# Turning the attention keys on the vector engine from a second, split read, in place of the tensor engine

## What is computed

```python
x = x + xattn(layernorm(x), ctx, ctx, Wq, bq, Wk, bk, Wv, bv)
#   qp = q @ Wq + bq; kp = ctx @ Wk + bk; vp = ctx @ Wv + bv
#   softmax(qp @ kp.T / sqrt(512)) @ vp
x = x + attn(layernorm(x), ...)     # q, k per head normalised, sigmoid gate, @ Wo + bo
x = x + ffn(layernorm(x), ...)      # one of 8 experts per row
```

## Time and profile before

| | |
|---|---|
| median of 3 runs | 393.93 us |
| span of the profiled execution, first to last instruction | 391.0 us |
| time of the runs less that span | 2.8 to 3.7 us, 2.9 for the median |
| PE busy | 363.3 us, 93% of the span |
| PE weight loads | 232.2 us |
| DVE busy | 147.2 us, 38% |
| ACT busy | 93.3 us, 24% |
| POOL busy | 82.2 us, 21% |
| moved by DMA | 56.48 MB in 13798 packets, mean 144 GB/s |

### The profile page before, as it was taken

The page is one execution under the profiler, slowest core; times in us unless marked ns, Lnnn a source line. Parts: engine busy times, 40 slices in busy tenths (PEclk is TensorE's granted clock), DMA queues, the critical chain, the costliest instruction groups (busy, mean ns, idle before and its releaser), DMA issues.

```text
span 391.0 us, 6077 instructions
## 1 busy us (share of the span) xinstructions
PE 363.3 (93%) x2346; PEld 232.2 (59%) x2346; DVE 147.2 (38%) x341; ACT 93.3 (24%) x191; POOL 82.2 (21%) x87
## 2 busy tenths in 40 slices
PE   1999999999999999999999999999889989799993
PEld 1786667435646544565654455653435869697781
DVE  4100365003616523351652444342362654155322
ACT  2222321213215331222541222241302400000000
POOL 4000243500215002022400201202322402511122
PEclk9999998999999999999999999999999999899998
DMA  7999200399700029710004950000693052920000
GB/s 256 409 404 351 93 0 2 107 341 373 309 2 0 2 80 382 264 27 0 0 0 174 380 200 0 2 0 2 230 421 157 3 214 71 324 104 18 29 24 25
DMA packets 13798, 56.48 MB, mean 144 GB/s; under 512 B 1574, under 2 KB 1606, under 8 KB 9680
## 3 DMA queue, kind: packets, MB, share of 16 engines
q1 hardware_dynamic: 11776, 50.35, 34.3%
q0 software_dynamic: 2000, 5.83, 4.2%
HBM read 53.03 MB, written 4.19 MB: 146 GB/s over the span
## 4 chain that ended last, share of the span: by engine, by line
PE 83%; DVE 6%; issue 3%; POOL 3%; ACT 2%; DMA 2%; DVEq 0%; ACTq 0%; POOLq 0%; SPq 0%
PE TR L911 14%; PE A L916 13%; PE ST L1005 12%; PE SC L982 12%; PE A L1191 8%; PE A L936 4%; PE A L958 4%; PE TR L916 4%; PE SC L1173 3%; PE A L911 2%; PE SC L1148 1%; DMA AW_sb<-rows,idxg_sb 1%; PE TR L992 1%; PE A L1123 1%; PE A L1053 1%
## 5 line engine op out<-in xcount | busy, mean ns | idle before, releaser
L260 DVE COPY CT_sb<-TR 128x512 f32<-128x512 f32 (+1 forms) x52 | 34.9, 672 | 64.5 <-PE TR L911 62.0
L911 PE MATMUL TR<-ident_sb,CTX_sb 128*128 128x128 f32 (+1 forms) x416 | 55.5, 274 | 3.4 <-ACT CT_sb L260 2.3
L911 PEld LDWEIGHTS TR<-ident_sb,CTX_sb 128*128 128x128 f32 (+1 forms) x416 | 44.5, 141 | 21.3 <-issue 13.9
L982 PE MATMUL SC<-CT_sb,qcur_sb 128*64 128x256 f32 x384 | 51.6, 391 | 0.0
L1005 PE MATMUL ST<-CTX_sb,PR_sb 128*64 128x512 f32 (+1 forms) x208 | 47.7, 599 | 0.9 <-ACT PR_sb L267 0.9
L260 ACT COPY CT_sb<-TR 128x512 f32<-128x512 f32 (+1 forms) x52 | 29.6, 569 | 63.4 <-PE TR L911 63.4
L982 PEld LDWEIGHTS SC<-CT_sb,qcur_sb 128*64 128x64 f32 x384 | 23.4, 136 | 14.5 <-issue 7.0
L1005 PEld LDWEIGHTS ST<-CTX_sb,PR_sb 128*64 128x64 f32 (+1 forms) x208 | 13.8, 136 | 24.4 <-issue 23.6
L916 PE MATMUL A<-AW_sb,normT_sb 128*128 128x512 f32 x48 | 22.0, 600 | 0.0
L399 POOL TENSOR_TENSOR rn_sb<-ss_sb,nhalf_sb 128x16 f32<-128x16 f32 x4 | 11.6, 2908 | 45.6 <-DVE ss_sb L709 45.6
L1148 PE MATMUL SC<-ident_sb 128*128 128x128 f32 x140 | 17.7, 278 | 0.0
(11 more groups left out here) (238 smaller groups left out, 488.0 us busy)
## 6 DMA issues: line engine op xcount, KB each, us to landing
CTX_sb<-ctx SPq DMA_DIRECT2D x24, 1024.0 KB, 8.2
CTX_sb<-wgu SPq DMA_DIRECT2D x4, 1024.0 KB, 9.4
CTX_sb<-wdn SPq DMA_DIRECT2D x5, 512.0 KB, 11.5
FF_sb<-wgu SPq DMA_DIRECT2D x2, 1024.0 KB, 14.1
rows<-XR_sb SPq DMA_DIRECT2D x3, 512.0 KB, 9.9
CTX_sb<-ctx SPq DMA_DIRECT2D x8, 130.0 KB
AW_sb<-x SPq DMA_DIRECT2D x2, 512.0 KB, 3.8
WQK_sb<-wq SPq DMA_DIRECT2D x1, 1024.0 KB, 8.2
```

The lines of the kernel that those rows point to most:

```text
L260: copy(ctxT[:, grp % 2, k, :, (t % GT) * P:(t % GT) * P + w], turned_bank(TR[k])[:, :, 0:w]).then_inc(s[f"moved{k}"], 1)
L911: last = t_.transpose(bank[:, c * w:c * w + n], rows[:, c * P:(c + 1) * P], ident[0:n, 0:n])
L982: last = t_.matmul(out[q, :], qcur[:, c, q], ctxT[:, grp % 2, k, c, 0:n], start=(c == 0), stop=(c == DC - 1))
```

## The change

PE no longer turns keys, and ACT and DVE no longer copy them out of PSUM. In their place the context is read a second time, into `split`, which lies in the space `FF` of experts 0 and 1. `split` has 3 slots of one group each. A group is read by 8 transfers (4 quadrants of 32 partitions x 2 batches) of 32 partitions x 8 blocks x 128 features, that is 512 bytes in one piece, 128 KB (131,072 bytes) each, 1.05 MB a group; the last group has 2 blocks and one more small transfer for the last key. DVE turns each group with two instructions (one for each batch) that transpose every 32x32 block and write straight to `CT`.

Turning within blocks leaves feature 4p + c on partition p of plane c, and `bring` takes every fourth column of `Wk` to match. The context rows for the weighted sum now come tile by tile (pieces of 2 KB, 8 KB before), so that both reads have their keys in one order. Experts 0 and 1 are loaded after the last keys are turned.

```diff
-MOVES = KT + NCH // 2
+MOVES = NCH // 2
+        split = FF[:, 0:NSPLIT * 2 * GT * D].rearrange("p (s k b d) -> p s k b d", s=NSPLIT, k=2, d=P)
...
-                    src = A["ctx"][bass.ds(b, 1), 0:FULL * P, :].rearrange("a (p t) d -> p (a t) d", t=FULL)[:, lo:hi, :]
+                    src = A["ctx"][bass.ds(b, 1), lo * P:hi * P, :].rearrange("a (t p) d -> p (a t) d", p=P)
...
+            def load_split(p, grp):
+
+                before_it = [(GROUPS - 1, 1), (4, 1), (5, 1)][grp] if grp < NSPLIT else (grp - NSPLIT, 0)
+                earlier(sp, "keysT_made", 2 * (GROUPS * (p - before_it[1]) + before_it[0] + 1))
+                slot, n = grp % NSPLIT, BLOCKS if grp < GROUPS - 1 else TAIL // Q
+                for quad in range(QUADS):
+                    for k in range(2):
+                        src = A["ctx"][bass.ds(2 * p + k, 1), grp * GT * P:grp * GT * P + n * Q, quad * P:(quad + 1) * P]
+                        sp.dma_start(split[quad * Q:(quad + 1) * Q, slot, k, 0:n, :],
+                                     src.rearrange("a (b r) d -> r (a b) d", r=Q)).then_inc(s_split[slot], 16)
...
+            for grp in range(5):
+                load_split(0, grp)
             load_pair(0)
...
             load_weight(awv, "awv", "av_in")
+            load_split(0, 5)
+            load_split(0, 6)
+            for grp in range(NSPLIT):
+                load_split(1, grp)
...
+            def rest_of_pair(p):
+                load_split(p, 3)
+                load_split(p, 4)
+                load_x(p)
+                load_split(p, 5)
+                load_split(p, 6)
+
+            with sp.Fori(1, PAIRS - 1) as p:
+                rest_of_pair(p)
+                for grp in range(NSPLIT):
+                    load_split(p + 1, grp)
+                load_pair(p + 1)
+                store_rows(p - 1)
+            rest_of_pair(PAIRS - 1)
+
+            sp.wait_ge(s["keysT_made"], 2 * GROUPS * PAIRS)
             for e in range(OWN):
                 load_expert(e)
...
+            def turn_keys(p, grp):
+
+                if grp >= GROUPS:
+                    return
+                slot, n = grp % NSPLIT, BLOCKS if grp < GROUPS - 1 else TBLOCKS
+                dve.wait_ge(s_split[slot], SPLIT_DMAS[slot][-1] * p + SPLIT_DMAS[slot][grp // NSPLIT])
+
+                earlier(dve, "scored", GROUPS * p + (grp - 1 if grp else 0))
+                for k in range(2):
+                    v.transpose(ctxT[:, grp % 2, k, :, 0:n * Q].rearrange("p c (b r) -> p b c r", r=Q),
+                                split[:, slot, k, 0:n, :].rearrange("p b (r c) -> p b c r", c=DC)).then_inc(s["keysT_made"], 1)
...
-                    last = t_.matmul(AB[m % 2][:, n], wkT[:, c, m * P:(m + 1) * P], qpT[:, c, n], start=(c == 0), stop=(c == DC - 1))
+                    last = t_.matmul(AB[m % 2][:, n], wkT[:, c, m:D:DC], qpT[:, c, n], start=(c == 0), stop=(c == DC - 1))
...
-                    for k in range(2):
-                        pe.wait_ge(s[f"moved{k}"], MOVES * p + min(lo + GT, KT))
+                    pe.wait_ge(s["keysT_made"], 2 * (GROUPS * p + grp + 1))
```

More of the change, by code:

```diff
@@ L16 @@
 GROUPS = -(-KT // GT)
+Q = 32
+QUADS = P // Q
+BLOCKS = GT * P // Q
+TBLOCKS = -(-TAIL // Q)
+NSPLIT = 3
+SPLIT_DMAS = [[16 * n for n in (8, 16, 25)], [16 * n for n in (8, 16)], [16 * n for n in (8, 16)]]
 CHUNKS = [(0, 4), (4, 8), (8, FULL), (FULL, KT)]
@@ L227, in program @@
         s_ctx = [[sem(f"ctx_in{k}{c}") for c in range(NCH)] for k in range(2)]
+        s_split = [sem(f"split_in{i}") for i in range(NSPLIT)]
         s_w = [sem(f"expert_in{e}") for e in range(E)]
@@ L265, in move_numerators @@
             w = P if c < NCH - 1 else TAIL
-            eng.wait_ge(s[f"turned{c % 2}"], MOVES * p + KT + c // 2 + 1)
+            eng.wait_ge(s[f"turned{c % 2}"], MOVES * p + c // 2 + 1)
             copy(probs[0:w, lo:hi, :], TR[c % 2][0:w, 0:(hi - lo) * P].rearrange("p (t q) -> p t q", q=P)).then_inc(s[f"moved{c % 2}"], 1)
@@ L569, in attention @@
                     a.activation(sm[:, 2:3], sm[:, 0:1], ACT.Exp, scale=-1.0).then_inc(s["en_made"], 1)
-            for t in range(KT):
-                if t == GT:
-                    move_qk(False, 0)
-                    move_qk(False, 1)
-                move_keys(act, a.copy, 0, 0, t)
+            move_qk(False, 0)
+            move_qk(False, 1)
             act.wait_ge(s["c_made"], 1)
@@ L584, in pair @@
             def pair(p, by_scores, by_max, by_sums):
-                for t in range(GT):
-                    move_keys(act, a.copy, p, 0, t)
                 for u in range(2 * GROUPS):
@@ L794, in _ @@
             dve.wait_ge(s["vec_in"], 16)
-            for t in range(GT):
-                move_keys(dve, v.tensor_copy, 0, 1, t)
+            turn_keys(0, 0)
+            turn_keys(0, 1)
             for u in range(2 * GROUPS):
@@ L810, in _ @@
                 move_numerators(dve, v.tensor_copy, 0, c)
+            turn_keys(1, 0)
+            turn_keys(1, 1)
             def pair(p, by_scores, by_max, by_sums):
-                for t in range(GT):
-                    move_keys(dve, v.tensor_copy, p, 1, t)
                 for u in range(2 * GROUPS):
@@ L828, in pair @@
                         attention(p - 1, step)
+                    if c >= 2 and not is_last(p):
+                        turn_keys(p + 1, c - 2)
             with dve.Fori(1, PAIRS - 1) as p:
@@ L997, in weigh @@
                 lo, hi = CHUNKS[c]
-                pe.wait_ge(s[f"moved{c % 2}"], MOVES * p + KT + c // 2 + 1)
+                pe.wait_ge(s[f"moved{c % 2}"], MOVES * p + c // 2 + 1)
                 if c == 0:
                     pe.wait_ge(s["exp_made"], NCH * (p + 1))
+                for k in range(2):
+                    pe.wait_ge(s_ctx[k][c], 16 * p + 16)
                 for t in range(lo, hi):
@@ L1091, in scores @@
             def scores(p, by_scores):
-                first = isinstance(p, int) and p == 0
-                if not first:
-                    turn_keys(p, 0)
-                turn_keys(p, 1)
-                if first:
+                if isinstance(p, int) and p == 0:
                     bring(False, 0)
```

37 lines of the change are left out of this document (9 added, 28 removed).

## The result

The changed kernel takes **447.46 us** (median of 4 runs, 445.91 to 448.25), the kernel before 393.88 us on the same chip: **1.137 times as long, 95% interval 1.133 to 1.140**. The forecast was 415 us in 388 to 447: slower as forecast, but the time lies 0.46 us above the range, and the loss is 53.6 us where 21 were forecast. The profiled execution has a span of 446.1 us (before 391.0). A few executions of later runs lie over 1.5% above the fastest of the same kernel; the ratios leave them out and the medians do not, and the traces of e7 and e16 are of such executions (431.87 us where the fastest took 424.71, 381.21 where it took 374.80).

A forecast was written before the change was run, and what follows sets the result against it. PE was taken to set the pace. Start +17.7, pair 1 0.0, pair 2 -0.8, last pair -3.4 and clock +7.6 make +21.1 on the 391.0 us span, 412.1; with 2.9 for the median 415 us, range 388 to 447.

The forecast's parts named there:

- The second read: DMA reading the context again into `split`: 5.3 us a group, the term said to decide; 3.8 us kept as an end.
- The chain that stood behind the turning: Second-layer steps across engines in a loop pair: PE's turning had filled their delays; pauses now 8.3 us a pair.
- the three named places: PE's pauses in a loop pair: 3.0 us at "on", 2.1 ahead of "a2", 2.2 behind the two masking copies.
- At nothing: Counted as free: ACT's 52 copies, later experts 0 and 1, 2 KB context rows, every fourth column of `Wk`.
- POOL's begin: At the start, `awk`, which POOL waits for, lands at 68.6 us behind five groups, instead of 42.08.
- the forecast's line: DMA price drawn through two queues: 0.0373 ns a byte and 22.6 ns fixed, so 512 bytes take 41.7 ns.
- DVE, what comes: 56 transposes replace 52 copies on DVE: 1.23 us per 1024 elements, 2.46 a group, some 30 us more work.
- rival C: DVE's transposes cost 2.7 us each because the source is read with a stride of 4 elements: 445 us, chance 0.12.
- Start: Pair 0: groups ahead of the weights delay its scores, so its sums begin at 92.05 instead of 74.35, +17.7 us.
- group 3's lateness: In later pairs group 3 lands behind the context rows: 4.2 us late in pair 2, 5.2 in pair 1.
- Clock: PE's clock falls to half speed after four long pauses, one in each pair, 1.9 us each: +7.6 us.

The follow-up runs named there:

- e7: e1 with pair 0's context rows and `wv` loaded behind groups 5 and 6 at the start: 431.25 us, 1.086 of the kernel before.
- e16: e13 with group 6 of the last pair issued ahead of all of its context rows: 378.09 us, 0.959 of the kernel before.
- e4: The changed kernel with plain copies for the transposes and the second read for pair 0 alone: 385.79 us, 0.982 of the kernel before.
- e1: The changed kernel with DVE reading its source without a stride and the columns of `Wk` laid out to match: 435.63 us.
- e5: The changed kernel with each transfer of a full group writing 128 partitions instead of 32, pieces still 512 bytes: 425.09 us, a single run.
- e3: The changed kernel with the second read made for pair 0 alone, later pairs turning what lies in the slots: 426.31 us.
- e13: e1 with pair 0 turned by PE as before, later pairs' groups 3 to 5 issued ahead of context rows, 6 ahead of their last part: 383.63 us.
- e2: The changed kernel with every transpose replaced by a plain copy of as many elements: 427.18 us, 1.087 of the kernel before.

## Why the prediction was partly right

**Right.** That it is slower, and by its second read. *The second read*, 5.3 us a group: 5.5. *The chain that stood behind the turning*: e4 leaves that chain with shorter turns, and its period is 57.2 with pauses of 1.05, 1.32 and 1.29 us at the three named places; after has them at the same places. *At nothing*: ACT's copies, the later experts and the strided columns of `Wk`. A weight load went from 203 to 323 ns, but most of it fell into the wait for group 5: the first 48 matmuls of `bring` took 12.99 us (8.97 in e1) long before it, and e1 begins its sums only 1.2 us earlier. *POOL's begin* at 68.6: `awk` came at 69.11.

**Right by luck.** The 5.3 us came from a price for each piece and each byte, whatever the partitions. By that line e5, with the same pieces over 128 partitions, would also need 5.3 us a group; it moves 290 GB/s, 3.6 us. So the forecast's line held the number and not the cause, of which the 32 partitions are the larger part. The 1.23 us for 1024 elements in order (1222 ns measured) came from a reduction and a copy out of PSUM; a plain copy of 1024 from SBUF takes 696 ns, so that line is no rule for DVE either.

**Failed: the term "DVE, what comes".** The stride of the source, which rival C named and the forecast dismissed ("no other operation here pays for its pattern"), made 1.23 us into 1.99. A group took 3.9 us instead of 2.46. The two pauses that hang on it grew: "on" 4.5 instead of 3.0, the masks 3.9 instead of 2.2.

**Failed: the term "Start"**, +17.7 against +25.1. `awv`, 1 MB, was left out between `awk` and group 5. Group 5 was turned from 78.01, not from 73.9; its turning took 3.86 instead of 2.46; PE did line 1145 (1123 before) and the last two `bring` calls in 13.5 us instead of 11.75. The clock was at half when group 5 was scored (the first of the two stretches below) and again in part of these calls (the second):

```profile
78.01 3.86 DVE L678 STREAM_TRANSPOSE CT_sb<-FF_sb 128x1024 f32<-128x1024 f32 x2 [5.70 <-DMA FF_sb<-ctx]
```

```profile
84.00:85.00 1.00, 1.00 (x8) 0.47 (x4) 1.00 (x2) 0.00 (x0) 1.00 (x1) 0.50 0.00 0
...
90.00:92.00 2.00, 2.00 (x7) 1.41 (x7) 0.55 (x4) 0.48 (x2) 0.19 (x1) 0.50 1.25 173
```

**Failed: group 3's lateness**, 4.2 us in pair 2 and 5.2 in pair 1. In after it looks nearly right: PE paused 8.77 us ahead of "a2" in pair 2, of which e3, without a late transfer, keeps 3.63, so 5.1 are the transfer's; in pair 1 the pause is 10.30, 6.7 of it lateness. But there the slow transposes bring DVE itself to group 3 late. In e1, where they have the forecast's price, DVE waits 7.7 us for group 3 in pair 2 and 13.07 in pair 1. The step behind it is when group 3 comes: its turn begins 21.0 us after the pair's start (the end of the sums before it) in after and 21.5 in e1, in pair 2, where 15.7 were forecast. That the issue hangs on group 6's turn, and that a longer pair so gives the DMA no more time, held: that turn ended 23.5 us before the end of pair 1 (23.4 by the forecast). From there to group 3's turn it took 44.5 us instead of 39.1. SP issues a store of 512 KB (line 314, at 195.00) between the rows and group 3, which the forecast left out, by estimate 1.4 us at 387 GB/s, and the rows went at 387 instead of 405 GB/s, 0.7 us; the rest was not taken apart.

**Failed, and the largest: the term "Clock", +7.6.** It counted four falls of 1.9 us. The same 1930 PE instructions are 338.6 us busy in after and 315.9 in e4, **22.7 us more**, and nearly all of it is clock, since both have the strided weight loads: by the sum over stretches of 1 us as above, 26.5 us of PE's busy time go with lower clock in after, 5.6 in e4 and 3.4 in before. In pairs 1, 2 and the last it is 8.2, 7.3 and 5.2 us, where the forecast had 1.9 each. From 100 to 260 us the granted clock is 1.00 in before and in e4, and 0.85 in after:

```profile
100.00:260.00 160.00, 121.78 (x626) 58.67 (x624) 86.34 (x125) 25.78 (x53) 25.06 (x20) 0.85 0.80 177
```

```profile
100.00:260.00 160.00, 148.29 (x857) 72.76 (x855) 73.18 (x178) 35.23 (x74) 35.65 (x27) 1.00 0.44 156
```

A pair has up to three falls, not one: behind "on", behind "a2" and behind the masks. The pauses that the forecast had there, 2 to 3 us, and the 4 us that two of them became, were taken as time only, since the rows had shown a fall after a longer idle time. Pauses of 3.6 to 4.4 us are enough, though not every one of them: e3 has no late transfer, and still 24.6 us of its busy time go with lower clock (8.4 in pair 1, 3.5 in pair 2). In e13 one of 2.10 us, ahead of "on" in pair 2, was followed by a clock of 0.50 from 152 to 154 us, while it stayed at 1.00 behind one of 2.14 us at 163.5. So a pause near 2 us can bring it down and need not.

How the parts combine was not foreseen either: e1 or e3 alone give 12 and 21 us, e2 and e3 together 62. The forecast had added terms that in part hide each other and in part feed the clock together. With the forecast's own price of a transpose (e1) the kernel still takes 435.6 us and not 415: the stride taken alone is the smaller part of the miss.
